# Mixture-of-experts combine: the residual x2 is added on GpSimd before VectorE's gated multiply-add, in place of a VectorE addition after it

## What is computed

```python
def _L0_ffn_ref(hidden_states, ...):
    top_v, top_i = jax.lax.top_k(probs, K)                 # K = 2 of E = 8 experts
    ...
    routed = jnp.einsum('te,etd->td', gates, out_e)        # two experts' rows per token, gated
    shared = ... / w1_s.shape[0]                           # the shared expert
    return alpha * shared + (1.0 - alpha) * routed         # alpha = 0.5
x = _layernorm(x + _L0_xattn_ref(x, ctx_1024, ctx_1024), axis=-1)   # this is x2
x = _layernorm(x + _L0_ffn_ref(x, ...), axis=-1)                    # the output
```

## Time and profile before

| what | value |
|---|---|
| median of 3 runs | 851.56 us |
| profiled execution, its own time | 843.65 us |
| its span | 841.9 us |
| busy: TensorE matmul, VectorE, ScalarE, GpSimd | 713.6, 487.4, 481.5, 461.6 us |
| combine: first gated multiply-add to last ACTIVATE | 766.90 to 837.93 us of the span |

### The profile page before, as it was taken

One profiled execution on the slowest core, in us unless ns is written; L12 is line 12 of the kernel. 1 busy time (PEld: TensorE's weight loads), 2 busy tenths in 40 slices (PEclk: granted clock), 3 DMA queues, 4 the chain that ended last, 5 costly groups with the idle time before them and its releaser, 6 DMA issues.

```text
span 841.9 us, 16996 instructions
## 1 busy us (share of the span) xinstructions
PE 713.6 (85%) x5112; PEld 650.7 (77%) x5113; DVE 487.4 (58%) x1435; ACT 481.5 (57%) x1441; POOL 461.6 (55%) x471
## 2 busy tenths in 40 slices
PE   5789999874999996898888888989889888999950
PEld 3668888763788885898888888888889887898750
DVE  3798999864899753433434343334333434446896
ACT  5889999821399722544445344445444444544796
POOL 3378988852111155266766666666666666541322
PEclk9999999875999997899999999999999999999985
DMA  5457555523211232011111111111111112215573
GB/s 172 151 176 227 176 181 168 151 75 102 74 51 51 76 84 64 24 41 42 44 44 41 44 41 44 44 44 41 41 44 44 44 42 42 38 58 154 149 217 109
DMA packets 87238, 72.57 MB, mean 86 GB/s; under 512 B 10067, under 2 KB 72411, under 8 KB 87195
## 3 DMA queue, kind: packets, MB, share of 16 engines
q1 hardware_dynamic: 77808, 53.43, 21.5%
q0 software_dynamic: 9088, 18.63, 8.3%
q10 hardware_dynamic: 298, 0.01, 0.0%
HBM read 50.14 MB, written 21.89 MB: 86 GB/s over the span
## 4 chain that ended last, share of the span: by engine, by line
PE 46%; issue 7%; DVE 5%; ACT 2%; another core or an unknown queue 1%; DMA 1%; ACTq 0%; POOLq 0%; POOL 0%; SPq 0%; DVEq 0%
PE bank L1325 15%; PE bank L1293 9%; PE bank L1294 9%; PE bank L1295 9%; PE bank L1285 2%; DVE xg L1609 2%; DVE f_st L1626 1%; DVE z L1620 1%; DVE f_hT L1597 1%; ACT xg L1571 1%; DMA f_x2T<-x2T_cols 1%; PE bank L1513 0%; PE bank L1512 0%; PE bank L1511 0%
## 5 line engine op out<-in xcount | busy, mean ns | idle before, releaser
L1403 DVE TENSOR_TENSOR e_hT<-e_sg,bank 128x512 f32<-128x512 f32 x142 | 97.7, 688 | 258.5 <-PE bank L1295 109.4
L1266 POOL DMA_INDIRECT y_rows<-e_y,dst_tab x142 | 148.0, 1042 | 108.5 <-ACT e_y L1357 75.8
L1293 PE MATMUL bank<-e_x_hi,e_w_hi 128*128 128x256 f32 x568 | 179.0, 315 | 29.9 <-issue 27.0
L1294 PE MATMUL bank<-e_x_lo,e_w_hi 128*128 128x256 f32 x568 | 167.1, 294 | 8.6 <-issue 7.8
L1295 PE MATMUL bank<-e_x_hi,e_w_lo 128*128 128x256 f32 x568 | 166.9, 294 | 4.2 <-issue 4.0
L1258 POOL DMA_INDIRECT xg<-x_rows,src_tab x130 | 130.1, 1001 | 55.1 <-issue 36.0
L1351 ACT ACTIVATE e_sg<-bank 128x512 f32<-128x512 f32 x142 | 84.6, 596 | 116.7 <-PE bank L1295 76.0
L1325 PE MATMUL bank<-w,e_hT 128*128 x1136 | 142.7, 279 | 4.7 <-issue 4.4
L1293 PEld LDWEIGHTS bank<-e_x_hi,e_w_hi 128*128 128x128 f32 x568 | 114.0, 201 | 37.1 <-issue 32.7
L1325 PEld LDWEIGHTS bank<-w,e_hT 128*128 128x128 f32 x1136 | 136.5, 196 | 6.0 <-issue 5.7
L1295 PEld LDWEIGHTS bank<-e_x_hi,e_w_lo 128*128 128x128 f32 x568 | 114.3, 201 | 9.5 <-issue 9.2
(11 more groups left out here) (172 smaller groups left out, 1544.2 us busy)
## 6 DMA issues: line engine op xcount, KB each, us to landing
yk<-y_rows SPq DMA_DIRECT2D x16, 512.0 KB, 4.4
xT_in<-in_xT_dram SPq DMA_DIRECT2D x16, 256.0 KB, 3.3
x_res<-in_x_dram SPq DMA_DIRECT2D x16, 256.0 KB, 3.6
w_in<-in_L_ffn_w_e_dram SPq DMA_DIRECT2D x16, 256.0 KB, 3.0
c_in<-in_ctx_dram SPq DMA_DIRECT2D x16, 256.0 KB, 2.9
cT_in<-in_ctxT_dram SPq DMA_DIRECT2D x16, 256.0 KB, 3.2
x_rows<-x SPq DMA_DIRECT2D x16, 256.0 KB, 2.4
x2T_cols<-x2T SPq DMA_DIRECT2D x16, 256.0 KB, 2.7
```

Of the source, the lines that this page charges most:

```text
L1266: nc.gpsimd.indirect_dma_start(y_rows, bass.IndirectOffsetOnAxis(dst_tab[:, n:n + 1], 0), y[b % R][:, t, :], None).then_inc(scattered[b % ...
L1293: nc.tensor.matmul(at, w_hi[r % 2][:, w], x_hi[r][:, :], start=True, stop=False)
L1294: nc.tensor.matmul(at, w_hi[r % 2][:, w], x_lo[r][:, :], start=False, stop=False)
L1403: nc.vector.tensor_tensor(hT[par][:, half * HC:(half + 1) * HC, :].rearrange("p c n -> p (c n)"), sg[half][:, :], bank[2 + half][:, :], AL ...
```

## The change

GpSimd gets a new step `with_x2(g)`: part = first + x2, on all 128 x 512 elements of a group. VectorE's `second(g)` is gone, and `total(g)` is now the gated multiply-add, gate1 * y1 + part, written to `z`; it stands where `second(g)` stood. The separate addition is gone. GpSimd's loop runs `with_x2(g)` ahead of `root(g - 1)`. A buffer of `yk` is now free when `z` is done.

```diff
         def load(g):
             if g >= R:
-                sp.wait_ge(part_ok, g - R + 1)
+                sp.wait_ge(z_ok, g - R + 1)
...
-        def second(g):
-            dve.wait_ge(first_ok, g + 1)
-            for t in range(GT):
-                last = nc.vector.scalar_tensor_tensor(part[g % 2][:, t, :], yk[g % R][:, t, 1, :],
-                                                      gates[:, 1, g * GT + t:g * GT + t + 1],
-                                                      first[g % 2][:, t, :], ALU.mult, ALU.add)
-            last.then_inc(part_ok, 1)
-
         def total(g):
             if g >= 4:
                 dve.wait_ge(res_ok, g - 3)
-            if g >= EARLY:
-                dve.wait_ge(added, g - EARLY + 1)
             dve.wait_ge(part_ok, g + 1)
-            nc.vector.tensor_tensor(z[g % R][:, :, :], part[g % 2][:, :, :],
-                                    x2_all[:, g * GT:(g + 1) * GT, :], ALU.add).then_inc(z_ok, 1)
+            for t in range(GT):
+                last = nc.vector.scalar_tensor_tensor(z[g % R][:, t, :], yk[g % R][:, t, 1, :],
+                                                      gates[:, 1, g * GT + t:g * GT + t + 1],
+                                                      part[g % 2][:, t, :], ALU.mult, ALU.add)
+            last.then_inc(z_ok, 1)
...
         for g in range(NG + 2):
             shared(LEAD + 2 * g)
             if g < NG:
-                second(g)
+                total(g)
             if 1 <= g <= NG:
                 spreads(g - 1)
             if g >= 2:
                 shifts(g - 2)
             shared(LEAD + 2 * g + 1)
-            if g < NG:
-                total(g)
             if 1 <= g <= NG:
                 moments(g - 1)
                 variances(g - 1)
...
+        def with_x2(g):
+            pool.wait_ge(first_ok, g + 1)
+            if g >= EARLY:
+                pool.wait_ge(added, g - EARLY + 1)
+            if g >= 2:
+                pool.wait_ge(z_ok, g - 1)
+            nc.gpsimd.tensor_tensor(part[g % 2][:, :, :], first[g % 2][:, :, :], x2_all[:, g * GT:(g + 1) * GT, :],
+                                    ALU.add).then_inc(part_ok, 1)
+
...
             while nx < LATE and FC * (nx - 1) + 1 < LEAD + 2 * g:
                 x_low(nx)
                 nx += 1
+            if g < NG:
+                with_x2(g)
             if g >= 1:
                 root(g - 1)
```

## The result

The changed kernel took 873.82 us in the median of 6 runs (870.28 to 878.81), the kernel before 850.71 in 6 runs beside and before them; the ratio is 1.0283, with a 95% interval of 1.0242 to 1.0324: 21 to 28 us slower. The profiled execution took 875.38 us, with a span of 873.6. Two executions beside the first four experiments, 1978.56 us of the kernel before and 1369.48 us of total_last, were far longer than all others and are left out of the ratios.

What follows compares the result with a forecast made beforehand. The prediction took TensorE's shared-expert chunks to bound rounds 0 to 8 and VectorE rounds 9 to 15. Lengthened rounds, 4.7 us against 2.99 at the end, summed to +19.7, rounded to +20 on 851.56: 872 us, range 866 to 882.

Steps and rivals of the forecast that it cites:

- The mechanism: In the combine, GpSimd's with_x2 and root and VectorE's round add up in series: rounds of 4.7 us against 2.99; chance 0.78.
- the sum: Start times of total(g) added round by round through the combine: total(15) at 849.8 instead of 830.12, +19.7 us.
- the "+3.5" of the range: GpSimd's with_x2 at 1.29 instead of 1.04 us adds 0.25 in 14 rings: +3.5 us.
- the hand-over to VectorE: In each combine round, from the end of GpSimd's with_x2 to VectorE's multiply-add: 0.03 us.
- The Trainium skill's price: For with_x2 on GpSimd, scaled from 4497 ns for 2048 elements to 512: 1.12 us, making the sum 1.1 us longer.
- TensorE's clock: Rival in the combine: gaps make TensorE's clock fall; for good from round 2, +40 us, 892 us; chance 0.10.
- Its short form: A short fall of TensorE's clock doubles one or two chunks of 2.29 us: up to 4 us more.
- GpSimd's work hidden: Rival: with_x2(g + 1) is done before VectorE reaches round g + 1; -3 us, 848.5 us; chance 0.05.
- The engines shutting each other out: Rival: GpSimd runs ahead and with_x2 meets a multiply-add each round; +6 us, 858 us; chance 0.04.
- Edits at nothing: Around the combine, load(g) released by z up to 3 us later, ScalarE's work, store queue and normalise(g - 4): no cost.
- Signs named ahead: Last multiply-adds 4.7 us apart, VectorE idle over 2 us before each, with_x2 near 1.04, VectorE about 10 us less busy.

Runs made afterwards that it cites:

- total_last: Changed kernel with VectorE issuing total(g) last in round g, behind variances(g - 1); ratio to the kernel before 1.0007, combine 75.33 us.
- wx_quarter: Changed kernel with GpSimd's addition on one of four tiles only, the gate waiting for z; ratio to the kernel before 1.0131, combine 85.75 us.
- total_mid: Changed kernel with VectorE's total(g) moved back behind the second hidden and add_shared; ratio to the kernel before 1.0139, combine 84.17 us.
- wx_ahead: Changed kernel with GpSimd issuing with_x2(g + 1) ahead of root(g - 1), VectorE's order kept; ratio to the kernel before 1.0114, combine 84.6 us.
- shift_late: total_last with VectorE's shifts(g - 2) moved behind moments(g - 1); ratio to the kernel before 0.9949, combine 72.98 us.

## Why the prediction was right, and where it was off

**The mechanism** was right: the loop of with_x2, total, variance, root, and again with_x2. It is shown from three sides: shortened (wx_quarter), shortened by order on VectorE (total_mid), opened (total_last). The forecast of 872 us and the measured 873.82 lie closer together than they deserve, since the kernel before came down from 851.56 to 850.71 with more runs: the forecast difference of +20 is just below the measured 21 to 28 and 4 us below the traces' 24.1, and the sum was short by that much.

**The sum, by its steps.** Counted from the first x_low, total(2) was forecast 15.7 us behind it and came at 16.1; total(8) 51.3, came at 53.9; total(15) 85.8, came at 90.3. Behind that 7.72 us instead of 7.8. The 4.5 us grow by 0.3 a round, nearly all from two terms:

- *with_x2* was set at 1.04, with 1.29 as the upper end. It took 1.27. The mis-sized step is the choice of the nearest row: I chose by output type (L454, L438), but what counts is that both operands are read in full, as in x_low (L965). 14 x 0.22 = 3.1 us, the "+3.5" of the range.
- *the hand-over to VectorE* was set at 0.03, from the shift behind the root. Behind with_x2 it is 0.10 (852.32 to 852.42): 14 x 0.07 = 1.0 us.

The other 0.4 us lie ahead of total(8), which starts 0.47 behind the end of its with_x2; why, the rows don't say. One reading was wrong and cost nothing: bn_aggr does not follow bn_stats directly, the shift stands between them (848.50, 849.28, 849.40), and the two together take the 0.90 us of the sum.

**The Trainium skill's price** (GPSIMD Engine Reference, "Elementwise — side-by-side cycle accounting") gave an estimate of 1.12 us, scaled from its figure for 2048 elements; 1.27 was measured, so it was too low by 0.15.

**TensorE's clock** stayed at 1.00 until 830 us, through stretches of 10 us in which it was busy 7.09 and 7.24: that rival did not happen in the changed kernel, as the sum had it. Its short form did in four of the experiments (total_mid, total_last, wx_ahead, shift_late): the clock was at 0.50 to 0.58 for a few microseconds, behind waits of TensorE for x_lo. **GpSimd's work hidden** did not happen here, but does in total_last; its condition, a root that doesn't hold the next with_x2, was named rightly. **The engines shutting each other out** did not happen in the changed kernel (multiply-adds 1.14, shifts 0.15), because the loop itself keeps them apart. It appears as soon as the loop opens. wx_ahead comes nearest to this rival, at +1.1% where I had put 0.7% (+6), but only 2.2 of its 10.7 us lie where the stretches are seen to set the round. There the shift and the variance were hit, and of 64 multiply-adds one (1.34, beside x_low), where I had looked at the multiply-add only.

**Edits at nothing**: load(g) released by z cost no wait on yk. Not free was what stands behind it in the queue: the late x2T load is issued after load(g), and x_high waited 5.4 us for it, where it was 3.6 before. In the changed kernel the loop hides that, as its rounds are longer than forecast by no more than the terms above; in shift_late it was worth 5 us, the fallen clock included.

**Signs named ahead**: rounds 4.98 and not 4.7; with_x2 1.27 and not near 1.04; idle before multiply-adds over 2 us, 2.44; root and with_x2 back to back; VectorE 487.4 to 475.5 us busy, 11.9 less.

## What to carry to other kernels

Before work goes to an idle engine, write down that engine's order beside the receiver's and look for a loop: if A's step waits for B and B's next one stands behind something that waits for A, both times add up and free time on B is worth nothing. Then the order is the change: the same instructions gave 1.028, 1.014, 1.001 and 0.995 by where one call stood, in the last case two. Moving the call on the other side (wx_ahead) gave 1.011, as it seems to have closed a new loop: write both lists down again for every order that you try. And where two engines shut each other out, even a four-element instruction can cost a microsecond; put it where the other engine does small work.

## What the runs showed of the hardware that was new to me

- A 128x512 f32 tensor-tensor on GpSimd takes 1.27 us with two full operands and 1.05 with one broadcast.
- A VectorE instruction of 128x4 with two SBUF inputs that starts while it runs, and a tensor_scalar from SBUF to SBUF, end only with it: 1.22, 1.07 and 0.84 us in place of 0.15 and 0.17. bn_stats, bn_aggr and the hidden product (one input in PSUM, 0.67 to 0.69) keep their time. The root on 4 elements, though it takes 1.01 us, stretches no multiply-add beside it (1.13 and 1.14).
- TensorE's granted clock fell from 1.00 to 0.50 in total_last behind an idle stretch of 2.65 us, and a chunk's eight down products then took 1.91 us in place of 1.05. In the changed kernel it stayed at 1.00 until the last chunk was done.
- The same program took 873.8 us in one set and 803.3 in another, with combines of 98.02 and 98.07 us. The stage ahead of it, the experts, makes the difference: from 400 to 500 us TensorE was busy 85.15 us in the one and 97.49 in the other. Why was not tried, and it need not be the chip: the record has the same chip number, 0, for a set with 842 us and one with 777.
